# Cross-attention kernel: halves of the first v projection, order of the first row of maxima, pieces of q around the fill's transposes

## What is computed

```python
q = split_heads(x @ Wq.T)          # x: 2 x 2048 x 640
k = split_heads(ctx @ Wk.T)        # ctx: 2 x 77 x 1024
v = split_heads(ctx @ Wv.T)
probs = softmax(q @ k.T * 32 ** -0.5)
out = merge_heads(probs @ v) @ Wo.T + bo + x
```

## Time and profile before

| | |
|---|---|
| median of three runs | 443.81 us |
| the profiled execution | 442.53 us, span 440.7 us |
| granted TensorE clock, mean | 0.998 |
| PE (matmul) busy | 428.6 us, 97% |
| DVE, ACT, POOL busy | 303.5, 252.4, 228.2 us (69%, 57%, 52%) |
| DMA moved | 72.70 MB, mean 165 GB/s |
| chain that ended last | PE 76%, POOL 7%, ACT 4%, issue 4%, DMA 4%, SP's queue 2%, DVE 1% |

### The profile page before, as it was taken

One profiled execution on the slowest core, in us unless ns is written; L12 is line 12 of the kernel. 1 busy time (PEld: TensorE's weight loads), 2 busy tenths in 40 slices (PEclk: granted clock), 3 DMA queues, 4 the chain that ended last, 5 costly groups with the idle time before them and its releaser, 6 DMA issues.

```text
span 440.7 us, 8273 instructions
## 1 busy us (share of the span) xinstructions
PE 428.6 (97%) x2538; PEld 311.8 (71%) x2538; DVE 303.5 (69%) x505; ACT 252.4 (57%) x509; POOL 228.2 (52%) x188
## 2 busy tenths in 40 slices
PE   8989988899999999999999999999999999999996
PEld 6977754577777767777777767777777767777675
DVE  0355796877768675967769675967769675966563
ACT  1728876757564565747565564747565564755510
POOL 7435777835655453645646453635646463634440
PEclk9999999999999999999999999999999999999999
DMA  8997433545345534555345534555344543444203
GB/s 285 356 360 260 148 106 123 194 144 170 122 150 184 169 122 161 186 178 173 120 147 175 175 128 147 184 178 186 122 150 164 166 144 123 160 152 168 74 24 120
DMA packets 39615, 72.70 MB, mean 165 GB/s; under 512 B 5024, under 2 KB 6176, under 8 KB 39584
## 3 DMA queue, kind: packets, MB, share of 16 engines
q1 hardware_dynamic: 28784, 52.62, 33.8%
q10 hardware_dynamic: 10800, 19.67, 13.9%
HBM read 28.81 MB, written 10.49 MB: 89 GB/s over the span
## 4 chain that ended last, share of the span: by engine, by line
PE 76%; POOL 7%; ACT 4%; issue 4%; DMA 4%; SPq 2%; DVE 1%; POOLq 0%; ACTq 0%; DVEq 0%
PE ps_o L694 24%; PE ps_q L694 23%; PE ps_s L740 9%; PE ps_pv L747 6%; PE ps_m L726 5%; POOL p_lo L337 4%; PE ps_den L752 3%; POOL x_lo L328 3%; DMA x_f<-in_x 2%; ACT p_f L435 2%; PE ps_o L678 1%; DMA wq_sb<-in_wq 1%; PE ps_m L791 1%; DMA q_packed<-mxT 1%; PE ps_m L731 1%
## 5 line engine op out<-in xcount | busy, mean ns | idle before, releaser
L337 POOL TENSOR_TENSOR p_lo<-p_f,p_hi 77x512 f16<-77x512 f32 x120 | 144.9, 1213 | 145.7 <-ACT p_hi L439 145.7
L435 ACT ACTIVATE p_f<-ps_s 77x512 f32<-77x512 f32 x160 | 94.9, 593 | 49.5 <-PE ps_s L740 49.5
L439 ACT ACTIVATE p_hi<-ps_s 77x512 f16<-77x512 f32 x160 | 93.8, 587 | 2.6 <-PE ps_den L752 2.6
L555 DVE TENSOR_REDUCE mx<-ps_m 128x4 f32<-128x308 f32 x160 | 69.0, 473 | 28.6 <-PE ps_m L726 28.2
L694 PE MATMUL ps_q<-x_hi,wq_hi 128*128 128x512 f32 x200 | 79.2, 396 | 1.7 <-DVE x_lo L543 0.7
L694 PE MATMUL ps_q<-x_lo,wq_hi 128*128 128x512 f32 x200 | 78.2, 391 | 0.0
L694 PE MATMUL ps_q<-x_hi,wq_lo 128*128 128x512 f32 x200 | 78.1, 391 | 0.0
L548 DVE TENSOR_TENSOR q_lo<-ps_q,q_hi 128x512 fp32r<-128x512 f32 x40 | 27.6, 689 | 66.4 <-ACT q_hi L418 66.4
L418 ACT CAST q_hi<-ps_q 128x512 fp32r<-128x512 f32 x40 | 23.4, 584 | 82.1 <-PE ps_q L694 82.1
L694 PE MATMUL ps_o<-attn_hi,wo_hi 128*128 128x512 f32 x170 | 69.5, 409 | 0.0
L694 PE MATMUL ps_o<-attn_hi,wo_lo 128*128 128x512 f32 x170 | 66.9, 393 | 0.0
(11 more groups left out here) (106 smaller groups left out, 597.3 us busy)
## 6 DMA issues: line engine op xcount, KB each, us to landing
q_packed<-q_hi SPq DMA_DIRECT2D x80, 256.0 KB, 2.5
x_f<-in_x SPq DMA_DIRECT2D x40, 256.0 KB, 3.1
q_packed<-q_lo SPq DMA_DIRECT2D x40, 256.0 KB, 3.1
x_res<-in_x ACTq DMA_DIRECT2D x35, 256.0 KB, 2.7
out<-out_sb ACTq DMA_DIRECT2D x35, 256.0 KB, 2.6
wk_sb<-in_wk SPq DMA_DIRECT2D x8, 320.0 KB, 5.6
wv_sb<-in_wv SPq DMA_DIRECT2D x5, 512.0 KB, 6.0
wq_sb<-in_wq SPq DMA_DIRECT2D x5, 320.0 KB, 5.7
```

What stands on the lines that cost most here:

```text
L337: nc.gpsimd.tensor_tensor(p_lo[:, i, :], p_f[:, i, :], p_hi[:, i, :], ALU.subtract).then_inc(plo_pool, 1)
L435: nc.scalar.activation(p_f[:, i, :], ps_s[i % 2][0:L, :], ACT.Exp, scale=SCALE).then_inc(pf_done, 1)
L439: nc.scalar.activation(p_hi[:, i, :], ps_s[i % 2][0:L, :], ACT.Exp, scale=SCALE).then_inc(phi_done, 1)
L555: nc.vector.tensor_reduce(mx[:, g % RS, :, tt], ps_m[tt % 2][:, 0:HG * L].rearrange("p (h k) -> p h k", k=L), AX_X, ALU.max).then_inc(max_ ...
```

## The change

- In step (-1, 4) `project_v(0)` is cut in two: chunks 0 to 3 first, then max products 0 and 1, chunks 4 to 7, max products 2 and 3, piece 0 of q, the transpose of maxima, piece 1, the transpose of v, pieces 2 to 4. ACT's `v_high` moves behind `copy_max` and DVE's `scale_v` behind the last two reductions in that step.
- `load_w(3)` and `load_w(4)` go from the ends of SP's steps (-1, 3) and (-1, 4) to steps (-1, 4) and (0, 0), there right behind the row of maxima.
- `query_group` is two ahead of the step where it was three. ACT casts wq groups 2, 3, 4 at the ends of steps (-1, 4), (0, 0), (0, 1), and POOL subtracts them at the heads of steps (0, 0), (0, 1), (0, 2); each was a step earlier. Group 1 stays ahead of the steps.
- In step (0, 0) piece 1 of q goes ahead of scores 3; in steps (0, 4) and (1, 0) it goes ahead of the transpose of maxima. Steps (0, 1) to (0, 3) keep their order on PE.

```diff
     def query_group(t, g):
-        return (nth(t, g) + 3,) if isinstance(t, int) and -2 <= nth(t, g) < G - 3 else ()
+        return (nth(t, g) + 2,) if isinstance(t, int) and 0 <= nth(t, g) < G - 2 else ()
...
             def step(t, g):
                 if exists(shift(t, g, 1)[0]):
                     load_max(*shift(t, g, 1))
+                if isinstance(t, int) and nth(t, g) in (-1, 0):
+                    load_w(nth(t, g) + G - 1)
...
                 if exists(shift(t, g, 2)[0]):
                     pack_q(*shift(t, g, 2))
-                if isinstance(t, int) and nth(t, g) in (-2, -1):
-                    load_w(nth(t, g) + G)
...
+            wq_low(1)
...
-                for v in value_group(t, g):
+                for v in value_group(t, g) if exists(t) else ():
                     v_high(v)
                 if exists(shift(t, g, 1)[0]):
                     copy_max(*shift(t, g, 1))
+                for v in value_group(t, g) if not exists(t) else ():
+                    v_high(v)
...
-                for v in value_group(t, g):
+                for v in value_group(t, g) if exists(t) else ():
                     scale_v(v)
                 if exists(t):
                     p_low(t, g, 0)
                 if exists(shift(t, g, 1)[0]):
                     reduce_max(*shift(t, g, 1), 2)
                     reduce_max(*shift(t, g, 1), 3)
+                for v in value_group(t, g) if not exists(t) else ():
+                    scale_v(v)
...
-            def project_v(g):
+            def project_v(g, chunks):
...
                 if (t, g) == (-1, G - 1):
+                    project_v(0, range(0, CC // 2))
                     pe.wait_ge(diag_done, HG)
-                    pe.wait_ge(klo_done, G)
+                    max_scores(max_t, max_g, 0, batch(max_t))
+                    max_scores(max_t, max_g, 1, batch(max_t))
+                    project_v(0, range(CC // 2, CC))
+                    max_scores(max_t, max_g, 2, batch(max_t))
+                    max_scores(max_t, max_g, 3, batch(max_t))
+                    project_q(*query, (0,))
+                    transpose_max(max_t, max_g)
+                    project_q(*query, (1,))
+                    transpose_v(0)
+                    project_q(*query, range(2, G))
+                    return
...
                 for v in value_group(t, g):
                     transpose_v(v)
-                if exists(t):
-                    scores(t, g, 3, batch(t))
-                before = 2 if value_group(t, g) else 1
-                project_q(*query, range(1, before))
+                if not exists(last_t):
+                    project_q(*query, (1,))
+                scores(t, g, 3, batch(t))
+                if exists(last_t):
+                    project_q(*query, (1,))
                 transpose_max(max_t, max_g)
-                project_q(*query, range(before, G))
+                project_q(*query, range(2, G))
```

More of the change, by code:

```diff
@@ L676, in project_v @@
                 pe.wait_ge(wv_in[g], 16)
-                for c in range(CC):
+                for c in chunks:
                     last = nc.tensor.matmul(ps_v, wv_sb[:, g, P * c:P * (c + 1)], ctx_sb[:, c, :],
                                             start=(c == 0), stop=(c == CC - 1))
-                last.then_inc(vproj_done, 1)
+                if CC - 1 in chunks:
+                    last.then_inc(vproj_done, 1)
             def transpose_v(g):
@@ L812, in fill @@
                 if (t, g) == (-1, G - 1):
+                    project_v(0, range(0, CC // 2))
                     pe.wait_ge(diag_done, HG)
-                    pe.wait_ge(klo_done, G)
+                    max_scores(max_t, max_g, 0, batch(max_t))
[9 more added lines that the diff above has]
+                    return
                 for v in value_group(t, g):
-                    project_v(v)
+                    project_v(v, range(CC))
                 if value_group(t, g):
@@ L834, in fill @@
                 max_scores(max_t, max_g, 3, batch(max_t))
-                if exists(t):
-                    scores(t, g, 2, batch(t))
+                scores(t, g, 2, batch(t))
                 for v in value_group(t, g):
                     transpose_v(v)
-                if exists(t):
-                    scores(t, g, 3, batch(t))
-                before = 2 if value_group(t, g) else 1
-                project_q(*query, range(1, before))
+                if not exists(last_t):
[3 more added lines that the diff above has]
+                    project_q(*query, (1,))
                 transpose_max(max_t, max_g)
-                project_q(*query, range(before, G))
+                project_q(*query, range(2, G))
             def step(t, g):
```

## The result

The changed kernel took **447.56 us** (median of four runs, 446.34 to 448.41), the kernel before 443.53 us (four runs). The ratio over all runs is 1.0102 (that of the two medians 1.0091), with a 95% interval of 1.0052 to 1.0153: slower, by 4.0 us in the medians and by 3.8 us between the two profiled executions (446.34 against 442.53 us, spans 444.5 and 440.7). The forecast was 446.3 us in a range of 445.3 to 449.0. The four runs of before lie between 440.74 and 443.94 us; in the later groups (22 and twice 27 runs) its median was 442.53 to 442.58, and set against that the loss is 5.0 us. Of the four runs of the changed kernel, the two at 446.34 and 446.85 us have a mean clock of 0.992, the two at 448.26 and 448.41 have 0.989 and 0.985; the profiled one is the fastest.

The account below looks back on a forecast made before the run. PE, full from 82.69 to 420 us, was taken to pass start-up changes on one for one. Terms -0.25 - 0.75 + 3.71 - 0.2 = +2.5 us on the median 443.81 gave 446.3 us, range 445.3 to 449.0.

Parts of the forecast that it names:

- the likeliest case: Whole kernel: the terms sum to +2.5 us, 446.3 us, with bounds 445.4 to 447.6; the forecast keeps 0.78.
- the rival with a chance of 0.10, the clock: After the stall in step (0, 2): clock falls, PE at half speed, +2.5 to +6.8 us, at most 450.6; chance 0.10.
- The stall: Step (0, 2): PE waits +3.71 us before q group 4 for POOL's wq_lo 4, behind both wo_lo; bounds 3.4 and 4.4.
- DVE gave way, so I add nothing: Stall in step (0, 2): POOL keeps its undisturbed time beside DVE's subtraction, nothing added; by the skill's rule some 4.4 us.
- matmul pace after the stall unchanged: Sign after the stall in step (0, 2): PE's matmuls keep the same pace.
- Step (-1, 4): v in halves: PE waits of 0.58 us in place of 0.71 + 0.14, -0.25 us (0 to -0.45).
- Step (0, 0): Row wait of 0.83 and exponential wait of 0.29 go, 0.37 added: -0.75 us (-0.4 to -1.1).
- this step's waits would stay as a whole: Step (0, 3): its 2.12 us of waits stay, as its chains hang on scores issued after the stall.
- a step (0, 3) under 11.75 us: Sign of being wrong: PE's step (0, 3) becomes shorter than 11.75 us.
- their rival (all of them vanish): Step (0, 3): DVE, ACT and POOL get ahead in the stall, 2.12 us of waits vanish: +0.4, 444.2 us; chance 0.06.
- Step (0, 4): Piece 1 ahead of the transpose covers 0.5 us, 0.3 comes back: -0.2 us (0 to -0.5).
- Step (1, 0): PE arrives 0.5 us earlier and waits 0.5 longer for POOL's p_lo in the next step: 0 (to -0.5).

Follow-up runs that it names:

- wq_first: Changed kernel with POOL subtracting the wq groups of each step at the end of the step before, wq_lo 4 thus ahead of wo_lo 0 and 1: 440.99 us, ratio 0.9961.
- b_wq_late: Kernel before with only POOL's wq_lo 4 moved to the head of step (0, 2), behind wo_lo 0 and 1: 448.16 us, ratio 1.0120.
- dve_late: Changed kernel with DVE's p_lo of step (0, 2) moved behind its last two reductions: 446.56 us, ratio 1.0072.
- pe_busy: Changed kernel with 16 thrown-away products on PE ahead of the wait for wq_lo 4: 444.13 us, ratio 1.0032.
- piece_after: The wq_first kernel with steps (0, 4) and (1, 0) in the old order, transpose of maxima ahead of piece 1: 441.22 us, ratio 0.9966.
- wq_between: Changed kernel with POOL's wq_lo 4 between wo_lo 0 and wo_lo 1: 443.73 us, ratio 1.0025.
- x_dve_attn: The wq_first kernel with x_lo 4 of tile 1 on DVE and, in step (1, 0), POOL's attn_lo 0 behind p_lo 2 and 3: 443.94 us, ratio 1.0033.
- first_again: The wq_first kernel unchanged, run again as the control: 441.08 us, ratio 0.9978.
- whole_v: The wq_first kernel with step (-1, 4) in the old order, v whole and its work ahead of that on maxima: 441.55 us, ratio 0.9979.
- row_behind: The wq_first kernel with loads of weight groups 3 and 4 back at the ends of steps (-1, 3) and (-1, 4): 443.57 us, ratio 1.0021.

## Why the prediction was right, and where it was not

**Direction, place and cause** were right: one wait for POOL's wq_lo 4 in step (0, 2), with wo_lo, wo_lo, wq_lo back to back, shown by wq_first from one side and by b_wq_late from the other. The time lay in the range. But that it did is in part luck. The forecast said +2.5 us and the medians say +4.0, at the upper edge of the likeliest case; the rival with a chance of 0.10, the clock, came true, and some 1.4 us of gains that the forecast did not have took most of its price back. The bounds of that case are also added wrongly: the terms' bounds together give 445.2 us (444.7 with that of step (1, 0)) to 447.8, not 445.4 to 447.6.

**The stall** was put at 3.71 us. By starts it was 53.59 - 49.47 = 4.12. The step that failed is "DVE gave way, so I add nothing": wq_lo 4 took 1.98 us in place of 1.54, and without DVE's subtraction beside it the stall is 3.67 (dve_late). The Trainium skill's rule that was weighed there ("SBUF — State Buffer", Who interferes with whom) was the better guide; by it the stall would have been 4.4, near the measured 4.1. One row in which POOL kept its pace was no proof that it always does, and step (0, 3) of the same trace had rows where it did not. DVE, then POOL, in the kernel before:

```profile
62.05 0.68 DVE L562 TENSOR_TENSOR p_lo<-p_f,p_hi 77x512 f16<-77x512 f32 x1
63.42 1.00 DVE L543 TENSOR_TENSOR x_lo<-x_f,x_hi 128x512 fp32r<-128x512 f32 x1
```

```profile
62.26 1.62 POOL L328 TENSOR_TENSOR x_lo<-x_f,x_hi 128x512 fp32r<-128x512 f32 x1 [3.08 <-ACT x_hi L389]
63.84 1.61 POOL L337 TENSOR_TENSOR p_lo<-p_f,p_hi 77x512 f16<-77x512 f32 x1
```

POOL's x_lo takes 1.29 us and its p_lo 1.16 in the median of that trace; each was some 0.4 longer here, beside a subtraction of DVE.

**The clock** was a rival and should have been a term: "matmul pace after the stall unchanged" failed. pe_busy prices it at 2.05 us, less than the 4.3 allowed for. With it and the longer stall the sum is 2.5 + 0.4 + 2.05 = 5.0, over the measured 3.8 by about what the points below return. The rule of the Trainium skill ("TensorE: Matmul & The Clock Gate", HAM oscillation) agrees here: the burst after the wait started at 0.50. In b_wq_late it did not: the burst began at full clock and the fall came 1.0 us later. The chance was set low because the trace of before had no such wait and, as the prediction has it, no clock below 1.00 after 20 us. That reading is wrong at the very end of the trace: PE's last product ends at 437.36 us, and the granted clock falls to 0.50 at 439.3 and stays there to the end, which accounts for the mean of 0.998. So an idle PE with full clock before it, and a fall 2.0 us later, stood in the trace. Its waits are not the same in every run either: b_wq_late, which starts as before does, waited 1.63 us for the row where the earlier trace rows have 0.83, and some runs of before have the lower clock. One profile shows one run.

**Step (-1, 4)**: -0.25 forecast; 28.33 - 21.00 = 7.33 against 7.61, so -0.28. Right.

**Step (0, 0)**: -0.75 forecast, -1.16 measured (7.95 us against 9.11). The row did not wait and the wq_lo wait was 0.3 by starts, as said. The terms removed were mis-sized: a bracket of idle time begins at the end of the last matmul's tail. By starts, the waits of 0.83 and 0.29 in the earlier trace rows stood for 0.99 and 0.43 of PE's time.

**Steps (0, 2) and (0, 3) gave back 0.8 us** that the forecast had at nothing. With the clock at full in pe_busy, (0, 2) after the stall is 4.61 us against 5.03, and (0, 3) is 11.34 against 11.75 in all of pe_busy, the changed kernel and b_wq_late. DVE's x_lo 0, which took 3.19 us in the earlier trace rows, fell between other subtractions of POOL and was short: 1.08 us in the changed kernel. That this is what shortens the step is read from the rows, and no run tried it. That this step's waits would stay as a whole was wrong by a fifth, and a step (0, 3) under 11.75 us was one of the prediction's own signs of being wrong: it did come. That their rival (all of them vanish) was unlikely was right.

**Step (0, 4)**: -0.2 forecast, -0.41 measured (7.23 against 7.64). The row did come late for (1, 0), by 0.26 us of starts, much as worked out; the wait that it covers was again worth 0.67 by starts, not 0.5. **Step (1, 0)**: nothing forecast in sum, nothing measured: the step is 0.37 us shorter, and the wait for p_lo behind it grew from 0.50 to 0.93. piece_after shows the same from the other side.

## What to carry to other kernels

When a producer is moved from one step to the next, read the program of its engine to the end of the step that it leaves: the work queued there now runs ahead of it, and the consumer waits for all of that. In these runs a stall of PE of 2 us or more nearly always cost more than its length, as the clock fell with it, and one of 1.4 us sometimes did; look at the granted clock behind every long wait, and at the end of the trace too, and price a wait by the starts of the matmuls around it. Where DVE and GpSimd each have a subtraction of two SBUF tiles due at once, leave gaps on the one that isn't urgent: here, back to back on GpSimd, they held DVE out for up to 5 us.

## What the runs showed of the hardware

The mean clock was lower in all runs of the kernels with a PE wait of 2.1 us (ten, wq_between), 3.4 (four, b_wq_late), 3.5 (three, dve_late) and 4.1 us (four, the changed kernel), and in nine of ten with 2.0 us (x_dve_attn). With 1.4 us as the longest wait it was lower in 3 of 11 (first_again), 4 of 11 (whole_v), 3 of 11 (piece_after), none of 6 (wq_first) and none of 9 (pe_busy, where the filled wait leaves the one of step (0, 3) as the longest); the first three were made on one chip and the last two on another. PE was full or nearly so on both sides of these waits. Where the profiles show the fall, it lies 1.7 us into the wait (the changed kernel), 1.5 into it (dve_late), 0.2 before its end (wq_between), or behind its end by 1.0 us (b_wq_late), 1.5 (x_dve_attn), and 0.4 and 0.2 for a wait of 1.4 us (piece_after, and the second fall of wq_between). With PE kept busy through the wait it did not fall, in nine of nine runs (pe_busy). Of PE's work, 3.2 to 3.4 us ran at 0.50 after a fall, but 4.5 and 4.7 in the changed kernel and dve_late. The price of a fall was 2.05 us by pe_busy, 1.5 to 2.7 us between runs of first_again, and 1.1 us for the second fall of wq_between. What decides in the case of 1.4 us stays open, the chip included; no run tried it.

DVE and GpSimd held each other up, but not in a fixed order: DVE's p_lo got its turn after one GpSimd subtraction (1.84 us for 0.68 of work, and 0.43 more for GpSimd), its attn_lo only after GpSimd's p_lo and row of three had ended (5.27 us). Over the whole trace of the kernel before, DVE's 16 attn_lo took 0.67 to 3.91 us with a median of 1.94, and GpSimd's 120 p_lo 1.15 to 1.62 with a median of 1.16: it is mostly DVE that loses time. What decides the turn was not tried.

An 8 KB DMA landed 4.4 us after its issue behind the weights of group 2 and the packs of q (the changed kernel), 3.3 us when it was issued 1.5 us later behind the same (whole_v), 4.9 behind the 832 KB of group 3 as well (row_behind); with little in flight (DMA share 0.02) it takes 1.8.
